# Which four of sixteen states are weighed on GpSimd: the fifth to eighth of a group, or the first four, with ScalarE copying their sum

## The chip, the cores and the metric

One core of one Trainium2 chip runs the whole program. Its engines are TensorE (PE, with its weight loads PEld), VectorE (DVE), ScalarE (ACT), GpSimd (POOL) and SyncE (SP), which here only issues DMAs. The metric is the device time of one execution in microseconds (us), lower is better.

## The reference, cut to what matters

Two adaLN layers over 2048 tokens of width 512. The first has a masked linear layer and a gated FFN. The second has a selective state-space block (the part that is changed) and a small mixture of LoRA experts. The state-space block, with D_IN = 1024 channels and N = 16 states:

```
dt = softplus(ts @ W_dt.T + b_dt)          # (tokens, 1024)
def step(state, inp):                      # over the tokens, in order
    dA = exp(dt_t[..., None] * A)
    state = state * dA + (dt_t * u_t)[..., None] * B_t[:, None, :]
    y = einsum('bdn,bn->bd', state, C_t)   # weigh the 16 states by C and add
    return (state, y)
y = ys + x * D
y = y * silu(gate)
return y @ W_out.T
```

## The kernel before, in words

Everything is written by hand: each engine has its own program, and semaphores order them. An engine runs its own program strictly in the order of the code.

Layer 0 takes the first part of the span. Layer 1 works on eight chunks of 256 tokens. In iteration i the state-space scan of chunk i runs, and between its steps lie pieces of the previous chunk p (out projection, router, experts) and of the next chunk n (norm, x projection, convolution, gates, dt). An iteration has 32 slots (`STEPS`): two groups g of four blocks of 128 channels, and 16 states in each. This text calls slot s of a group, counted from its start, st; the first group's slots are 0 to 15 of the iteration, the second's 16 to 31. In each slot:

- POOL multiplies `dbu = dtu * b_all` for all four blocks (L1851) and adds the folded carry into two columns (L1855). It may be up to four slots ahead of the scans (`AHEAD`).
- ACT makes the decay `exp(dt * A)` in two halves (L1612) and between them copies the last column of the previous state into `carry` (L1625); then it does the pieces that its function `others` lists for the slot before.
- DVE runs two scans (L2023), one for each half, into `h[:, s % RING]`, of which there are three.
- PE transposes the state into the two banks `ps_h`, one for each 128 tokens (`turn_h`, L1411), and DVE then adds it, weighed by C, to the sum `acc` (`add_state`, L2041; for a group's first state L2038, which sets `acc`). This follows one slot behind the scan.

Four states of each group, st 4 to 7, go another way (`on_pool`): POOL multiplies the state by a broadcast C in place (`weigh_h`, L1873, three slots behind its scan and behind that slot's `dbu`), and PE adds the transposes of all four into `ps_h` itself (`add_h`, L1399), together with D times u (`init_acc`, L1387). DVE then adds that sum to `acc` once (`join_acc`, L2050). Meanwhile states 8 and 9 wait for the banks. DVE has no add in st 5 to 8, the sum in st 9 and two adds in st 10; PE turns state 10 at the end of its slot 10, behind the x projection of that slot.

A buffer `h` comes free when PE has turned it: the scan of slot s waits for the transposes of slot s - 3. DVE's `rms_apply` (L2088, L2091) in slot 22 waits for POOL's `rms_pow` (L1907, L1909), which stands behind the `dbu` of slot 24.

## Time and profile before

| | |
|---|---|
| Times of three runs | 1701.98, 1704.54, 1706.6 us (median 1704.54) |
| The profiled execution | 1702.61 us, of which its span is 1700.8 us |
| DVE busy over the span | 1300.6 us (76%) |
| PE busy over the span | 1421.5 us (84%) |
| POOL busy over the span | 1079.5 us (63%) |
| ACT busy over the span | 891.7 us (52%) |
| Chain that ended last | PE 28%, POOL 20%, DVE 14%, issue 6%, ACT 3% |

Busy is the time in which the engine ran an instruction; the rest of the span it waited or had nothing to do. The shares are averages over layer 0 and layer 1, which have different limits. A group of rows gives the count and the mean time of its instructions; a row of the timeline gives start, duration, line, output <- inputs, and in brackets how long the engine was idle before it and for whom it waited.

### The profile page before, as it was taken

What the parts mean: (1) busy time and instruction counts of PE and PEld (TensorE: products, weight loads), DVE (VectorE), ACT (ScalarE), POOL (GpSimd) and SP (SyncE); (2) the same over time, 40 slices, a digit from 0 to 9 for tenths busy, and PEclk for the clock granted to TensorE, in tenths of its full rate; (3) what the DMA queues carried; (4) which work ended last, traced back from release to release, by engine and by line L of the source; (5) the groups of instructions that cost most, each with busy time, mean ns of one, the idle gap of its engine ahead of it and who ended that gap; (6) DMA issues with size and microseconds to landing.
All of it is one profiled execution on the core that took longest, in us unless ns stands there. A gap on an engine that the chain in (4) does not pass through costs nothing.

```text
span 1700.8 us, 25246 instructions
## 1 busy us (share of the span) xinstructions
PE 1421.5 (84%) x8781; PEld 1010.4 (59%) x8781; DVE 1300.6 (76%) x1746; ACT 891.7 (52%) x2369; POOL 1079.5 (63%) x958
## 2 busy tenths in 40 slices
PE   6789999999997785987898789788788878977677
PEld 5566766777765564665476456456546645745443
DVE  5685655554422898988989989898898998989983
ACT  3333333243215657656666665765666566575441
POOL 0352332322232969968977995996897699599780
PEclk9699999999999898999999999999999999999587
DMA  9421221111001002001100200110110030010001
GB/s 313 154 100 54 78 100 50 50 32 32 26 30 63 1 1 72 16 1 51 50 1 14 87 1 1 60 41 1 51 50 1 2 99 1 1 63 26 1 0 38
DMA packets 32579, 77.20 MB, mean 45 GB/s; under 512 B 3826, under 2 KB 4914, under 8 KB 31940
## 3 DMA queue, kind: packets, MB, share of 16 engines
q1 hardware_dynamic: 32452, 75.59, 13.1%
q8 instruction: 70, 1.15, 0.3%
q14 instruction: 57, 0.47, 0.1%
HBM read 66.99 MB, written 8.59 MB: 44 GB/s over the span
## 4 chain that ended last, share of the span: by engine, by line
PE 28%; POOL 20%; DVE 14%; issue 6%; ACT 3%; DVEq 0%; POOLq 0%; ACTq 0%
POOL dbu L1851 10%; DVE h L2023 7%; PE ps_h L1411 6%; POOL h L1873 5%; DVE acc L2041 3%; PE ps_m L1374 3%; PE ps_o L1435 2%; PE ps_m L159 2%; PE ps_m L1350 2%; PE ps_m L161 2%; PE ps_m L160 2%; PE ps_h L1399 2%; ACT ps_a L1612 2%; POOL dt L1917 1%; PE ps_s L1374 1%
## 5 line engine op out<-in xcount | busy, mean ns | idle before, releaser
L1851 POOL TENSOR_TENSOR dbu<-dtu,b_all 128x1024 f32<-128x1024 f32 x256 | 603.6, 2358 | 144.7 <-DVE h L2023 131.8
L2023 DVE TENSOR_TENSOR_SCAN h<-ps_a,carry,dbu 128x512 f32<-128x512 f32 x512 | 627.4, 1268 | 47.3 <-PE ps_h L1399 33.3
L1612 ACT ACTIVATE ps_a<-dt,a_neg 128x256 f32<-128x256 f32 (+1 forms) x1024 | 442.9, 465 | 238.6 <-DVE h L2023 238.2
L1411 PE MATMUL ps_h<-ident,h 128*128 128x128 f32 x1536 | 243.6, 303 | 125.5 <-DVE acc L2041 91.3
L1411 PEld LDWEIGHTS ps_h<-ident,h 128*128 128x128 f32 x1536 | 189.7, 155 | 193.8 <-DVE h L2023 107.4
L2041 DVE SCALAR_TENSOR_TENSOR acc<-ps_h,c_cur,acc 128x512 f32<-128x512 f32 x352 | 246.2, 740 | 34.2 <-PE ps_h L1411 33.5
L709 POOL TENSOR_TENSOR hid_l<-hid,hid_h 128x256 f16<-128x256 f32 (+1 forms) x88 | 77.2, 880 | 158.4 <-ACT hid_h L600 158.3
L1873 POOL TENSOR_TENSOR h<-h,c_all 128x1024 f32<-128x1024 f32 x64 | 150.6, 2352 | 23.1 <-ACT carry L1625 22.8
L159 PE MATMUL ps_m<-h_h,wi_h 128*128 128x256 f16 x440 | 125.5, 285 | 47.2 <-DVE u L2069 23.0
L592 ACT ACTIVATE sil<-ps_gu 128x256 f32<-128x256 f32 (+1 forms) x88 | 33.9, 385 | 180.9 <-PE ps_gu L161 180.9
L161 PE MATMUL ps_m<-h_h,wi_l 128*128 128x256 f16 x440 | 125.7, 286 | 0.0
L160 PE MATMUL ps_m<-h_l,wi_h 128*128 128x256 f16 x440 | 125.2, 284 | 0.0
L1435 PE MATMUL ps_o<-wo,y 128*128 128x512 f32 x224 | 108.5, 613 | 3.1 <-DVE x L2127 2.9
L1399 PE MATMUL ps_h<-ident,h 128*128 128x128 f32 x512 | 70.4, 282 | 34.4 <-POOL h L1873 34.1
L159 PE MATMUL ps_gu<-h_h,g_h 128*128 128x256 f16 (+1 forms) x352 | 96.6, 274 | 1.7 <-DVE u_l L998 1.0
L161 PE MATMUL ps_gu<-h_h,g_l 128*128 128x256 f16 (+1 forms) x352 | 96.5, 274 | 0.0
L160 PE MATMUL ps_gu<-h_l,g_h 128*128 128x256 f16 (+1 forms) x352 | 96.5, 274 | 0.0
L159 PE MATMUL ps_gu<-h_h,u_h 128*128 128x256 f16 (+1 forms) x352 | 96.1, 273 | 0.0
L160 PE MATMUL ps_gu<-h_l,u_h 128*128 128x256 f16 (+1 forms) x352 | 96.1, 273 | 0.0
L161 PE MATMUL ps_gu<-h_h,u_l 128*128 128x256 f16 (+1 forms) x352 | 96.1, 273 | 0.0
L1374 PE MATMUL ps_m<-xw,diag_t 128*128 128x256 f32 x384 | 91.1, 379 | 0.0
L1625 ACT ACTIVATE carry<-h 128x4 f32<-128x4 f32 x255 | 52.7, 207 | 70.9 <-DVE h L2023 70.5
(334 smaller groups left out, 2838.5 us busy)
## 6 DMA issues: line engine op xcount, KB each, us to landing
b_all<-bt_scratch SPq DMA_DIRECT2D x32, 512.0 KB, 4.0
wm<-in_wmod SPq DMA_DIRECT2D x7, 1024.0 KB, 6.5
wo<-in_wmod SPq DMA_DIRECT2D x5, 1024.0 KB, 9.1
xa<-in_x SPq DMA_DIRECT2D x8, 512.0 KB, 4.5
stage<-in_W_in SPq DMA_DIRECT2D x4, 1024.0 KB
x_scratch<-x SPq DMA_DIRECT2D x8, 512.0 KB, 3.1
c_all<-bt_scratch SPq DMA_DIRECT2D x8, 512.0 KB, 3.5
x<-x_scratch SPq DMA_DIRECT2D x8, 512.0 KB, 3.6
```

Source lines behind the costliest of these rows:

```text
L159: pe.matmul(out, lh, rh, start=(first and k == 0), stop=False)
L160: pe.matmul(out, lh, rl, start=False, stop=False)
L161: mm = pe.matmul(out, ll, rh, start=False, stop=(last and k == n - 1))
L1374: pe.matmul(x_bank(m), diag_t[:, m, tap], xw[:, m % 2, tap:tap + CH], start=(tap == 0), stop=False)
L1399: tr = pe.matmul(ps_h[:, t, j * P:(j + 1) * P], h[:, s % RING, j, t * P:(t + 1) * P], W["ident"][:], is_transpose=True, start=(begin and j ...
L1411: tr = pe.transpose(ps_h[:, t, j * P:(j + 1) * P], h[:, s % RING, j, t * P:(t + 1) * P], W["ident"][:])
L1435: mm = pe.matmul(ps_o[:], y[:, k, tok], W["wo"][:, k], start=(k == 0), stop=(k == KI - 1))
L1612: ex = nc.scalar.activation(ps_a[:, j, j % 2:], dt[:, m, j % 2:], ACT.Exp, scale=a_neg[:, m, st:st + 1])
L1851: nc.gpsimd.tensor_tensor(dbu[:, s % AHEAD], dtu[:, g * DG:(g + 1) * DG], b_all[:, st, :].unsqueeze(1).to_broadcast([P, DG, CH]), ALU.mult ...
L1873: nc.gpsimd.tensor_tensor(h[:, s % RING], h[:, s % RING], c_all[:, s % NS - C_FROM, :].unsqueeze(1).to_broadcast([P, DG, CH]), ALU.mult).t ...
L2023: nc.vector.tensor_tensor_scan(h[:, s % RING, two].rearrange("p j t -> p (j t)"), ps_a[:, two].rearrange("p j t -> p (j t)"), dbu[:, s % A ...
L2041: op = nc.vector.scalar_tensor_tensor(part, ps_h[:, t], c_t, part, ALU.mult, ALU.add)
```

## The change

The weighed states are now the first four of each group, st 0 to 3. PE adds state 0 in slot 1, state 1 in slot 3, state 2 in slot 4 and state 3 in slot 5, each time near the end of the slot (`ADD_AT`); `init_acc` is in slot 3. ACT copies the sum of the two banks into `acc` (`join_acc`, after the exponentials of slot 6), so `acc` starts with it: the product that set `acc` and DVE's add of the sum are both gone, and state 0 no longer needs either. DVE adds state 4 at the end of slot 6, states 5 and 6 in slot 7, and from slot 8 on one a slot as before. There are four buffers `h` instead of three. To make place, `dtu` holds one group instead of two: POOL makes the second group's in slot 15 behind its `dbu`, and the next chunk's first half in slot 31 (before: slots 5 and 30). Some small pieces of ACT and POOL move by a few slots. The scratch in DRAM holds 20 rows of B and C a chunk in place of 24.

```
-C_FROM = 4
-C_TO = C_FROM + KC
+ADD_AT = {1: 0, 3: 1, 4: 2, 5: 3}
+JOIN_AT = 5
...
-    RING = 3
+    RING = 4
...
-    dtu = sb("dtu", [P, KI, CH], F32, c)
+    dtu = sb("dtu", [P, DG, CH], F32, c)
...
     def on_pool(s):
-        return C_FROM <= s % NS < C_TO
+        return s % NS < KC
...
         def turn_h(i, s):
             pe.wait_ge(S["scan_half"], half_at(i, s, 1))
             for t in range(TT):
-                bank_free(i, use_of_step(s), t, first)
+                bank_free(i, use_of_step(s), 1 if s % NS == KC else t, False)
...
-                if st < C_FROM:
-                    turn_h(i, s, first)
-                elif st in (C_TO + 1, C_TO + 2):
-                    turn_h(i, s - 1, False)
-                elif st > C_TO + 2:
-                    turn_h(i, s, False)
+                if st == JOIN_AT + 1:
+                    turn_h(i, s - 2)
+                elif st == JOIN_AT + 2:
+                    turn_h(i, s - 1)
+                elif st > JOIN_AT + 2:
+                    turn_h(i, s)
...
-                if st == C_TO - 1:
+                if st in ADD_AT:
+                    add_h(i, s - st + ADD_AT[st], first)
+                if st == 3:
                     init_acc(i, s // NS)
-                if C_FROM < st <= C_TO:
-                    add_h(i, s - 1)
-                if st == C_TO + 2:
-                    turn_h(i, s, False)
+                if st == JOIN_AT + 1:
+                    turn_h(i, s - 1)
+                if st == JOIN_AT + 2:
+                    turn_h(i, s)
...
+        def join_acc(i, g, first):
+
+            if not first:
+                act.wait_ge(S["y_mm"], (i - 1) * (KI // 2) + (g + 1) * (DG // 2))
+            for t in range(TT):
+                act.wait_ge(S["hT_done"], turned_at(i, use_of_join(g), t))
+                nc.scalar.activation(acc[:, t, g * DG * P:(g + 1) * DG * P], ps_h[:, t], ACT.Copy).then_inc(S["hT_used"], 1)
...
             if s == 0:
                 keep_c(i, first)
+            if s % NS == JOIN_AT:
+                join_acc(i, s // NS, first)
...
-            if s == 5:
+            if s == 8:
                 first_decay(i, 1)
-            if s == 6:
+            if s == 9:
                 d_u(i, 1)
...
+            pool.wait_ge(S["db_mul"], (n * 2 + g) * NS)
+            nc.gpsimd.tensor_tensor(dtu[:], dt[:, grp], u[:, grp], ALU.mult).then_inc(S["dtu_done"], 1)
...
-            if s == 3:
+            if n is not None and s == 3:
+                inv_std_a(n - 1)
+            if s == 7:
                 dt_add(i, 1, first)
-            if n is not None and s == 4:
-                inv_std_a(n - 1)
-            if s == 5:
-                dt_u(i, 1)
...
-            if s == 8:
+            if s == 12:
                 fold_carry(i, 1, first)
+            if s == NS - 1:
+                dt_u(i, 1)
...
-        def join_acc(i, g):
-            use = use_of_join(g)
-            for t in range(TT):
-                dve.wait_ge(S["hT_done"], turned_at(i, use, t))
-                dve.wait_ge(S["hT_used"], i * (USES * TT) + (use * TT + t - 1))
-                part = acc[:, t, g * DG * P:(g + 1) * DG * P]
-                nc.vector.tensor_tensor(part, ps_h[:, t], part, ALU.add).then_inc(S["hT_used"], 1)
...
+            if m == DG and not first:
+                dve.wait_ge(S["dtu_done"], n * 2)
...
-                if st == C_TO + 1:
-                    join_acc(i, s // NS)
...
-                if st == C_TO + 2:
+                if st == JOIN_AT + 2:
                     add_state(i, s - 2)
-                elif (st <= C_FROM or st > C_TO + 2) and not (first and s == 0):
-                    add_state(i if s else i - 1, (s - 1) % STEPS, first)
+                elif (st == 0 or st > JOIN_AT + 2) and not (first and s == 0):
+                    add_state(i if s else i - 1, (s - 1) % STEPS)
...
-                if st == C_TO + 2:
+                if st == JOIN_AT + 1:
+                    add_state(i, s - 2)
+                if st == JOIN_AT + 2:
                     add_state(i, s - 1)
```

The order of three engines' instructions shows where the work stands now. Line numbers of after differ: L2035 is the scan, L2048 the weighed add, L2089 and L2092 `rms_apply`, L2076 a gate's product; on POOL L1863 and L1867 are `dbu`, L1885 `weigh_h`, L1919 and L1921 `rms_pow`.

DVE in the second group before, from `rms_apply` in slot 22 to the two adds of slot 26:

```order
L2088 TENSOR_TENSOR ssn<-ps_s,rms 128x2x32
L2091 TENSOR_TENSOR ssn<-ps_s,rms 128x32 x2
L2023 SCALAR_TENSOR_TENSOR h<-ps_a,carry,dbu 128x512 x2
L2075 SCALAR_TENSOR_TENSOR sg<-th,ps_m 128x256
L2023 SCALAR_TENSOR_TENSOR h<-ps_a,carry,dbu 128x512 x4
L2050 TENSOR_TENSOR acc<-ps_h,acc 128x512 x2
L2023 SCALAR_TENSOR_TENSOR h<-ps_a,carry,dbu 128x512 x2
L2041 SCALAR_TENSOR_TENSOR acc<-ps_h,c_cur,acc 128x512 x4
```

And now, from the same `rms_apply` in slot 22 to the adds of slot 23:

```order
L2089 TENSOR_TENSOR ssn<-ps_s,rms 128x2x32
L2092 TENSOR_TENSOR ssn<-ps_s,rms 128x32 x2
L2048 SCALAR_TENSOR_TENSOR acc<-ps_h,c_cur,acc 128x512 x2
L2035 SCALAR_TENSOR_TENSOR h<-ps_a,carry,dbu 128x512 x2
L2048 SCALAR_TENSOR_TENSOR acc<-ps_h,c_cur,acc 128x512 x2
L2076 SCALAR_TENSOR_TENSOR sg<-th,ps_m 128x256
L2048 SCALAR_TENSOR_TENSOR acc<-ps_h,c_cur,acc 128x512 x2
```

The stretch without adds ended four slots behind `rms_apply` and now ends with it, and the DVE's add of the sum is gone.

POOL in the second group before, from the first `weigh_h` to the second:

```order
L1873 TENSOR_TENSOR h<-h,c_all 128x1024
L1921 TENSOR_TENSOR gap<-top 128x2
L1922 CAST at<-top_at 128x4
L1851 TENSOR_TENSOR dbu<-dtu,b_all 128x1024
L1855 TENSOR_TENSOR dbu<-dbu,fold 128x2
L1907 TENSOR_SCALAR mse<-msq 128x6
L1909 TENSOR_TENSOR rms<-mse,mhalf 128x6
L1873 TENSOR_TENSOR h<-h,c_all 128x1024
```

And now, from the fourth `weigh_h` on:

```order
L1885 TENSOR_TENSOR h<-h,c_all 128x1024
L1863 TENSOR_TENSOR dbu<-dtu,b_all 128x1024
L1867 TENSOR_TENSOR dbu<-dbu,fold 128x2
L1933 TENSOR_TENSOR gap<-top 128x2
L1934 CAST at<-top_at 128x4
L1863 TENSOR_TENSOR dbu<-dtu,b_all 128x1024
L1867 TENSOR_TENSOR dbu<-dbu,fold 128x2
L1919 TENSOR_SCALAR mse<-msq 128x6
L1921 TENSOR_TENSOR rms<-mse,mhalf 128x6
```

`rms_pow` stood behind one weighing of the group and now stands behind all four.

PE in the first group before, from the norm's transposes in slot 3 to the out projection of slot 6 (L1286 turns the norm, L1435 is the out projection):

```order
L1286 MATMUL ps_s<-ident,xn 128x128 x4
L1435 MATMUL ps_o<-wo,y 128x512 x2
L1286 MATMUL ps_m<-ident,xn 128x128 x4
L1435 MATMUL ps_o<-wo,y 128x512 x4
L1399 MATMUL ps_h<-ident,h 128x128 x8
L1435 MATMUL ps_o<-wo,y 128x512 x2
```

And now, with the states' transposes among them:

```order
L1286 MATMUL ps_s<-ident,xn 128x128 x4
L1435 MATMUL ps_o<-wo,y 128x512 x2
L1399 MATMUL ps_h<-ident,h 128x128 x8
L1387 MATMUL ps_h<-ident,ab 128x128 x8
L1286 MATMUL ps_m<-ident,xn 128x128 x4
L1435 MATMUL ps_o<-wo,y 128x512 x2
L1399 MATMUL ps_h<-ident,h 128x128 x8
L1435 MATMUL ps_o<-wo,y 128x512 x2
L1399 MATMUL ps_h<-ident,h 128x128 x8
L1411 MATMUL ps_h<-ident,h 128x128 x8
```

The transposes that free the buffers `h` now stand behind the out projections of the first group, where there were none in between.

## Rows read from the trace of the kernel before

**Rows 1.** The page's busy times over the whole span.

```profile
PE 1421.5 (84%) x8781; PEld 1010.4 (59%) x8781; DVE 1300.6 (76%) x1746; ACT 891.7 (52%) x2369; POOL 1079.5 (63%) x958
```

**Rows 2.** Windows: six iterations, chunks 1 to 6, from join to join.

```profile
723.95:1571.00 847.05, 691.87 (x4159) 488.80 (x4158) 760.59 (x972) 542.30 (x1490) 698.42 (x591) 0.96 0.09 30
```

**Rows 3.** Waits of DVE in that stretch: total, times, longest.

```profile
DVE acc L2041 <- PE ps_h L1411: 29.1, 24, 3.6
DVE h L2023 <- PE ps_h L1399: 23.5, 16, 2.4
DVE acc L2050 <- PE ps_h L1399: 16.7, 12, 1.8
```

**Rows 4.** Groups by line over the span: busy us, mean ns | idle before.

```profile
L2023 DVE TENSOR_TENSOR_SCAN h<-ps_a,carry,dbu 128x512 f32<-128x512 f32 x512 | 627.4, 1268 | 47.3 <-PE ps_h L1399 33.3 <-ACT ps_a L1612 5.5 <-ACT carry L1625 5.4
...
L2041 DVE SCALAR_TENSOR_TENSOR acc<-ps_h,c_cur,acc 128x512 f32<-128x512 f32 x352 | 246.2, 740 | 34.2 <-PE ps_h L1411 33.5
...
L2038 DVE TENSOR_SCALAR acc<-ps_h,c_cur 128x512 f32<-128x512 f32 x32 | 22.3, 740 | 0.0
...
L2050 DVE TENSOR_TENSOR acc<-ps_h,acc 128x512 f32<-128x512 f32 x32 | 20.7, 686 | 23.2 <-PE ps_h L1399 23.2
```

**Rows 5.** Timeline of DVE in chunk 3's first group, slots 8 to 11.

```profile
999.02 2.46 DVE L2023 TENSOR_TENSOR_SCAN h<-ps_a,carry,dbu 128x512 f32<-128x512 f32 x2 [0.64 <-ACT carry L1625]
...
1003.63 2.46 DVE L2023 TENSOR_TENSOR_SCAN h<-ps_a,carry,dbu 128x512 f32<-128x512 f32 x2 [1.57 <-PE ps_h L1399]
1007.26 1.29 DVE L2050 TENSOR_TENSOR acc<-ps_h,acc 128x512 f32<-128x512 f32 x2 [1.17 <-PE ps_h L1399]
1008.46 1.28 DVE L2054 BATCH_NORM_STATS2 stats<-x 128x6 f32<-128x512 f32 x2
...
1014.88 1.41 DVE L2041 SCALAR_TENSOR_TENSOR acc<-ps_h,c_cur,acc 128x512 f32<-128x512 f32 x2 [0.70 <-PE ps_h L1411]
...
1022.62 1.41 DVE L2041 SCALAR_TENSOR_TENSOR acc<-ps_h,c_cur,acc 128x512 f32<-128x512 f32 x2 [3.65 <-PE ps_h L1411]
```

**Rows 6.** Timeline of DVE in chunk 2's second group, slots 24 to 27.

```profile
930.46 2.46 DVE L2023 TENSOR_TENSOR_SCAN h<-ps_a,carry,dbu 128x512 f32<-128x512 f32 x2 [0.54 <-PE ps_h L1399]
935.36 2.46 DVE L2023 TENSOR_TENSOR_SCAN h<-ps_a,carry,dbu 128x512 f32<-128x512 f32 x2 [2.44 <-PE ps_h L1399]
939.63 1.29 DVE L2050 TENSOR_TENSOR acc<-ps_h,acc 128x512 f32<-128x512 f32 x2 [1.81 <-PE ps_h L1399]
940.84 2.45 DVE L2023 TENSOR_TENSOR_SCAN h<-ps_a,carry,dbu 128x512 f32<-128x512 f32 x2
```

**Rows 7.** Timeline of POOL in the same stretch.

```profile
924.82 0.19 POOL L1855 TENSOR_TENSOR dbu<-dbu,fold 128x2 f32<-128x2 f32 x1
...
926.76 2.35 POOL L1873 TENSOR_TENSOR h<-h,c_all 128x1024 f32<-128x1024 f32 x1
929.06 2.36 POOL L1851 TENSOR_TENSOR dbu<-dtu,b_all 128x1024 f32<-128x1024 f32 x1
...
931.65 2.35 POOL L1873 TENSOR_TENSOR h<-h,c_all 128x1024 f32<-128x1024 f32 x1
```

**Rows 8.** Timeline of ACT in chunk 3, slots 6 and 7.

```profile
993.89 0.57 ACT L1635 ACTIVATE h_h<-ps_m 128x512 f16<-128x512 f32 x1
...
996.44 1.69 ACT L1696 ACTIVATE ab<-u,d_vec 128x256 f32<-128x256 f32 x4
```

**Rows 9.** Timeline of PE in chunk 2, slots 17 to 19.

```profile
909.33 3.92 PE L1350 MATMUL ps_m<-u,wx 128*64 128x256 f32 x16
913.19 1.10 PE L1411 MATMUL ps_h<-ident,h 128*128 128x128 f32 x8
...
918.06 1.09 PE L1411 MATMUL ps_h<-ident,h 128*128 128x128 f32 x8
```

**Rows 10.** Windows: chunk 3's slots 18 to 20 (PEclk is the third figure from the end).

```profile
1050.00:1065.00 15.00, 14.76 (x103) 10.34 (x103) 13.82 (x23) 6.83 (x21) 8.04 (x10) 0.89 0.01 2
```

More of the change, by code:

```diff
@@ L1389, in init_acc, with add_h @@
             tr.then_inc(S["init_done"], 1)
-        def add_h(i, s):
-            begin, last = s % NS == C_FROM, s % NS == C_TO - 1
+        def add_h(i, s, first):
+            begin, last = s % NS == 0, s % NS == KC - 1
             pe.wait_ge(S["hc_done"], on_pool_before(i, s) + 1)
@@ L1396, in add_h @@
                 if begin:
-                    bank_free(i, use_of_join(s // NS), t, False)
+                    bank_free(i, use_of_join(s // NS), t, first)
                 for j in range(DG):
@@ L1404, in add_h, with turn_h @@
                 tr.then_inc(S["hc_used"], 1)
-        def turn_h(i, s, first):
+        def turn_h(i, s):
             pe.wait_ge(S["scan_half"], half_at(i, s, 1))
             for t in range(TT):
-                bank_free(i, use_of_step(s), t, first)
+                bank_free(i, use_of_step(s), 1 if s % NS == KC else t, False)
                 for j in range(DG):
@@ L1710, in tsb_in @@
             act.wait_ge(S["tsb_mm"], n + 1)
-            nc.scalar.activation(tsb[0:RDT + NS + C_TO, :], ps_s[0:RDT + NS + C_TO, 0:CH], ACT.Copy).then_inc(S["tsb_done"], 1)
+            nc.scalar.activation(tsb[0:RDT + NS + KC, :], ps_s[0:RDT + NS + KC, 0:CH], ACT.Copy).then_inc(S["tsb_done"], 1)
         def router_in(p):
@@ L1850, in db @@
                 pool.wait_ge(S["scan_half"], i * (2 * STEPS) + 2 * (s - AHEAD + 1))
-            nc.gpsimd.tensor_tensor(dbu[:, s % AHEAD], dtu[:, g * DG:(g + 1) * DG],
+            nc.gpsimd.tensor_tensor(dbu[:, s % AHEAD], dtu[:],
                                     b_all[:, st, :].unsqueeze(1).to_broadcast([P, DG, CH]), ALU.mult).then_inc(S["db_mul"], 1)
@@ L1967, in others @@
                 weigh(p)
-            if s == 8:
+            if s == 12:
                 fold_carry(i, 1, first)
+            if s == NS - 1:
+                dt_u(i, 1)
             if n is not None and s == STEPS - 3:
                 dt_add(n, 0)
-            if n is not None and s == STEPS - 2:
+            if n is not None and s == STEPS - 1:
                 dt_u(n, 0)
-            if n is not None and s == STEPS - 1:
                 fold_carry(n, 0)
@@ L2026, in scans, with add_state @@
                                              carry[:, s, 2 * half:2 * half + 1], ALU.mult, ALU.add).then_inc(S["scan_half"], 1)
-        def add_state(i, s, first=False):
+        def add_state(i, s):
             g, st, use = s // NS, s % NS, use_of_step(s)
-            if st == 0 and not first:
-                dve.wait_ge(S["y_mm"], (i - 1) * (KI // 2) + (g + 1) * (DG // 2))
             for t in range(TT):
@@ L2036, in add_state @@
                 c_t = c_cur[:, t, st:st + 1]
[L2037 to L2050 removed]
+                dve.wait_ge(S["hT_used"], i * (USES * TT) + (use * TT + t - 1))
+                op = nc.vector.scalar_tensor_tensor(part, ps_h[:, t], c_t, part, ALU.mult, ALU.add)
+                op.then_inc(S["hT_used"], 1)
         def statistics(n, src, st, ag):
@@ L2064, in low, with make_u @@
                                     ALU.subtract).then_inc(lo, 1)
-        def make_u(n, m):
+        def make_u(n, m, first=False):
             dve.wait_ge(S["tanh_done"], value(n, KI, m))
+            if m == DG and not first:
+                dve.wait_ge(S["dtu_done"], n * 2)
             nc.vector.scalar_tensor_tensor(u[:, m], th[:, m % 2], 1.0, x_bank(m), ALU.add, ALU.mult).then_inc(S["u_done"], 1)
@@ L2116, in first_dt @@
             dve.wait_ge(S["dt_done"], 1)
-            nc.vector.tensor_tensor(dtu[:, 0:DG], dt[:, 0:DG], u[:, 0:DG], ALU.mult).then_inc(S["dtu_done"], 1)
+            nc.vector.tensor_tensor(dtu[:], dt[:, 0:DG], u[:, 0:DG], ALU.mult).then_inc(S["dtu_done"], 1)
         def make_y(i, m):
@@ L2209, in _ @@
         for m in range(KI):
-            make_u(0, m)
+            make_u(0, m, True)
         mean_squares(0)
```

30 lines of the change are left out of this document (12 added, 18 removed).

## The prediction, made before the changed kernel ran

> **What bounds the kernel now.** I read the page's busy times first, then windows over the six alike iterations, then the waits of VectorE in that stretch, and last the timelines of single groups. Over the whole span VectorE is busy 76% and POOL 63% [rows 1], which is a mean over two layers. In the six iterations of chunks 1 to 6 the reader should see another picture: 847.05 us, of which VectorE works 760.59 and POOL 698.42 [rows 2]. An iteration takes 141.2 us, with 126.8 us of VectorE's work, and 86.5 us / 6 = 14.4 us in which it waits. So VectorE bounds layer 1, and a change is worth what it takes from its work plus what it takes from these 14.4 us. The waits have three main names: the weighed add behind PE's transposes (29.1 us), the scan behind `add_h` (23.5) and the join behind `add_h` (16.7) [rows 3]. All three belong to the stretch in which four states are weighed.
>
> Why it waits there: POOL needs 929.06 - 926.76 = 2.30 us for a weighing and 931.65 - 929.06 = 2.59 us for a slot's `dbu` with its small add [rows 7], so 4.89 us for a slot with both. VectorE needs 2.37 us for a slot's two scans, and has no add there. Its scans start 935.36 - 930.46 = 4.90 us apart [rows 6]: POOL's pace. With three buffers `h` the scan of slot s also waits for the weighing of s - 3 and PE's eight transposes behind it.
>
> **The change, part by part.** I count from T, the end of a group's first scan. The first weighing starts at T + 0.5.
>
> *Work.* The join on VectorE goes: 1008.46 - 1007.26 = 1.20 us a group [rows 5]. Setting `acc` goes, but state 0 to 3 are weighed now and all twelve others are added; before it was one set and eleven adds, and both kinds take 740 ns [rows 4]. So only the join counts: 16 x 1.20 = 19.2 us, of it 2.4 in each iteration.
>
> *The join on ACT.* The nearest row is a copy of one bank in 0.57 us, to half-width numbers [rows 8]; I take 0.6 each, 1.2 for two. Bounds: 0.5 and 0.75 each. Behind it on ACT stand a gate's tanh or the copy of the norm (slot 5's list), and the exponentials of slot 7, and VectorE's scan waits for those.
>
> *Fourth buffer.* A scan now waits for the weighing of s - 4, which stands on POOL ahead of this slot's own `dbu`. So where PE is in time the fourth buffer leaves `dbu` as the bound.
>
> *First group.* POOL: four weighings (9.2), the `dbu` of slots 4 to 7 (10.4), the norm's small steps (1.5): the fourth weighing ends at T + 19.0. VectorE until then has its statistics (1.5), the last add (1.3), five scans (11.8), two products y, four gates and others: some 19 us, so it hardly waits on POOL. PE has four gate tiles, four out projections of 1.7 to 1.9 us, and the transposes behind them. By my walk through the slots the third `add_h` ends at 20.1, where the scan of slot 6 waits 0.75 us for it, and the fourth at 22.8. ACT waits for that, copies until 23.6 and then copies the norm until 24.2, which VectorE needs in slot 6: 1.65 us. ACT's normalise and `d_u` (1.69 us [rows 8]), which now meet slots without an add, cost 0.25 and 0.45; the turn of state 7 behind an out projection and an x tile 0.3. With some 0.6 for latencies that is 4.0 us. Before it was 0.64 + 1.57 + 1.17 + 0.70 + 3.65 = 7.7 us [rows 5]. The 3.65 is PE's turn of state 10, which stood behind an x tile that waits for VectorE's own slot 11; now the late turns are those of states 5 and 7, ahead of any tile that waits so.
>
> *Second group.* VectorE has an add, u, and y in slots 16 to 18. PE turns y, does `wx` in 3.92 us [rows 9] and reaches the first `add_h` at T + 10.9; then a gate tile and the router (3.6 us, between the transposes at 913.19 and 918.06 [rows 9]). ACT takes the router's output at 14.8 and tanh after it, so VectorE waits 1.8 us in slot 20 for the gate. The scans of slots 21 and 22 wait 0.6 and 0.65 for `add_h`, the gate of slot 22 another 1.25 (tanh stands behind the join on ACT). Then comes `rms_apply`. POOL's `rms_pow` stood behind one weighing and now stands behind four: 0.5 + 4 x 2.30 + 5 x 2.59 + 0.3 (`gap`) + (926.76 - 925.0 = 1.7) [rows 7] = T + 24.7. VectorE is ready at 24.7 after those waits, so this costs nothing more, but if the others shrink it is what comes late next: it ends the stretch at T + 24.7 in any case. PE turns state 20 at 25.05, and the add of it starts at 25.2. The waits sum to 1.8 + 0.6 + 0.65 + 1.25 + 0.3 + 0.5 = 5.1. Before, this group and the rest of the iteration had 14.4 - 7.3 = 7.1 us (the first group varies by some 1 us over the chunks), of which 0.54 + 2.44 + 1.81 stand in [rows 6].
>
> *PE's clock.* In slots 18 to 20 the granted clock is 0.89 of full over 15 us [rows 10], so the array ran about 3.3 us of it at 1.2 GHz and the rest at 2.4, after a wait. PE now waits some 3 us ahead of the second y of slot 17. I put 1.0 us an iteration on it (between 0, since the row shows that one such drop is there already, and 1.65, half of 3.3). The Trainium skill, "TensorE: Matmul & The Clock Gate", Part 1, says that the array falls to half its rate when it has been idle and comes back after it was kept busy. By that rule there would be a drop in each second group inside the critical stretch; at the upper bound the sum would be 4 us less of a gain. The row agrees that there are drops, not where the new ones would lie.
>
> *Moved without cost.* `dtu` in slots 15 and 31 (2.36 us of POOL) stands right ahead of the next group's first `dbu`, and that is needed four slots later; POOL runs its work from slot 16 to the next slot 3 without a pause by T + 62.3, and VectorE is there at T + 64.4. Were that cover gone, each would cost up to 2.4 us. The new wait of u(4) for `dtu` has 6 us of slack. ACT's dt steps in slots 24 to 28 no longer lie in a stretch at POOL's pace; 1.2 us for these and the experts' late sum.
>
> **The sum.** Waits in an iteration: 4.0 + 5.1 + 1.0 + 1.2 = 11.3 for 14.4, so -3.1; work -2.4; together -5.5, times six -33. The first and the last chunk bring their four joins, -4.8, and I give their waits nothing. That is -37.8 on the profiled execution of 1702.61 us: 1664.8. The median lies 1.9 higher, so 1666. For this kernel 0.3%, or 5 us, is about what can be told from no change.
>
> **The rivals.**
> - *Only the work goes.* The waits move but stay 14.4 us: the join chain (fourth weighing, transposes, ACT's copy, turn, add) takes the place of `add_h` and VectorE's join. For it: the chain has one more engine in it. Against: 3.65 us had a cause of its own. 1704.5 - 19 = 1685. Chance 0.25.
> - *The waits fall to 8 us.* PE and ACT get through without the small waits and only the POOL-bound end is left. Another 3.3 x 6 = 20 us: 1647. Chance 0.10.
> - *PE is late.* The transposes that free `h` and open the banks stand behind gates, router and out projections. PE's stretch from the second y to the fourth `add_h` is 17.8 us long and ends only 0.15 us ahead of need, so every further us there is one of VectorE's. From 5.5 us an iteration on it decides. Were the stretch wholly at 1.2 GHz it would be about 12 us longer: 7 x (12 - 5.5) = +45, 1750. For it: short light slots now hold the same PE work. Against: over the six iterations the clock is 0.96 [rows 2] and PE has 155 us free. Slower in some such way: 0.07, mostly at 1712 to 1730.
> - *Nothing measurable*: gain and PE's lateness cancel, 1704. Chance 0.05.
>
> **How the numbers follow.** The forecast, 1655 to 1678, has 0.53. With the first rival above it and half of the second below, 1647 to 1692 holds somewhat over 8 in 10. Faster by over 0.3% is the forecast and the first two rivals: 0.53 + 0.25 + 0.10 = 0.88; same 0.05; slower 0.07.
>
> **What would show it.** VectorE's busy time falls by about 22 us (the joins' 20.7 [rows 4]). The six iterations take 135 to 137 us each, with 11 us of waiting; the 3.65 us wait of the eleventh slot is gone. A new wait of `rms_apply` for POOL's `rms` or just under it appears in slot 22, and one for ACT in slots 6 and 20. The scans' waits for PE shrink to the small ones of slots 6, 21 and 22. I am wrong if the waits of add and scan together are as large as before, if ACT's join starts later than T + 25, or if POOL shows no waits for scans in slots 26 to 31 and its `dbu` makes the scans wait.

## The result: 1660.87 us, and the profile after

| | before | after |
|---|---|---|
| Times | 1701.98 to 1706.6 us, median 1704.18 (4 runs) | 1657.41 to 1664.34 us, median 1660.87 (4 runs) |
| Profiled execution, its span | 1702.61, 1700.8 us | 1660.69, 1658.5 us |
| Granted clock over the span | 0.937 | 0.943 |

The ratio is 0.9746, with a 95% interval of 0.9721 to 0.977: 43 us faster. 1666.0 was forecast, with a range of 1647 to 1692.

First the page's busy times, which answer to [rows 1]:

```profile
PE 1399.8 (84%) x8781; PEld 1000.2 (60%) x8781; DVE 1281.2 (77%) x1714; ACT 900.7 (54%) x2401; POOL 1078.1 (65%) x958
```

VectorE works 1300.6 - 1281.2 = 19.4 us less, in 32 instructions fewer. The span fell by 42.3 us. So more than half of the gain is waiting that went, and it must be looked for in the six alike iterations.

For these I take the same mark in both kernels, `rms_apply` in slot 22 (L2088 before, L2089 after), which stands once in each of chunks 0 to 6. This is the view of one line's instructions, with the first and the last start; from the one to the other are six iterations. The first row is of the kernel before, the second of the one after:

```profile
L2088 DVE TENSOR_TENSOR ssn<-ps_s,rms x7: 224/225/228, 645.5 to 1493.5; 128x64 f32<-128x64 f32 x7
```

```profile
L2089 DVE TENSOR_TENSOR ssn<-ps_s,rms x7: 216/217/225, 643.6 to 1460.8; 128x64 f32<-128x64 f32 x7
```

An iteration fell from 848.0 / 6 = 141.3 us to 817.2 / 6 = 136.2. The windows between these marks, before and after (the second answers to [rows 2]; after the times and the counts of the five engines stand the clock, the DMA share and GB/s):

```profile
645.50:1493.50 848.00, 691.14 (x4182) 493.39 (x4180) 761.98 (x978) 545.62 (x1500) 697.54 (x586) 0.95 0.09 30
```

```profile
643.60:1460.80 817.20, 681.86 (x4177) 490.41 (x4178) 749.09 (x953) 551.73 (x1521) 698.55 (x586) 0.95 0.10 31
```

The third engine is VectorE: its work fell by 12.9 us, 2.15 an iteration, and its waiting from 86.0 to 68.1 us, so from 14.3 to 11.35 an iteration. The clock stayed at 0.95. What it waits for now, in the same window of the kernel after (answers to [rows 3]):

```profile
DVE sg L2076 <- ACT th L1668: 18.3, 17, 1.8
DVE h L2035 <- ACT carry L1627: 15.6, 18, 1.9
DVE h L2035 <- PE ps_h L1399: 15.4, 24, 0.9
DVE h_l L2062 <- ACT h_h L1637: 7.9, 6, 1.5
DVE x L2128 <- PE ps_o L1435: 5.1, 5, 1.0
DVE acc L2048 <- PE ps_h L1411: 2.9, 13, 0.3
```

Two of the three names of [rows 3] are all but gone: the weighed add waited 29.1 us and now waits 2.9, and the join's 16.7 went with the join. The third, the scans behind `add_h`, is at 15.4. In their place ScalarE is named, for 41.8 us in all: a gate's tanh (L1668), the carry (L1627) and the fp16 copy (L1637).

The two places where these waits lie, on VectorE, first the first group of chunk 4 (its T is 1091.4; answers to [rows 5]):

```profile
1100.22 0.42 DVE L2076 SCALAR_TENSOR_TENSOR sg<-th,ps_m 128x256 f32<-128x256 f32 x1 [0.32 <-ACT th L1668]
1101.08 2.46 DVE L2035 TENSOR_TENSOR_SCAN h<-ps_a,carry,dbu 128x512 f32<-128x512 f32 x2 [0.44 <-ACT carry L1627]
...
1108.48 0.69 DVE L2128 TENSOR_TENSOR x<-ps_o,x 128x512 f32<-128x512 f32 x1 [1.01 <-PE ps_o L1435]
1109.52 2.46 DVE L2035 TENSOR_TENSOR_SCAN h<-ps_a,carry,dbu 128x512 f32<-128x512 f32 x2 [0.35 <-PE ps_h L1399]
...
1113.42 2.46 DVE L2035 TENSOR_TENSOR_SCAN h<-ps_a,carry,dbu 128x512 f32<-128x512 f32 x2 [0.86 <-PE ps_h L1399]
1117.15 0.69 DVE L2062 TENSOR_TENSOR h_l<-ps_m,h_h 128x512 f16<-128x512 f32 x1 [1.27 <-ACT h_h L1637]
```

Then the second group of chunk 3 (T is 1024.95; answers to [rows 6]):

```profile
1037.79 2.46 DVE L2035 TENSOR_TENSOR_SCAN h<-ps_a,carry,dbu 128x512 f32<-128x512 f32 x2 [1.94 <-ACT carry L1627]
1042.10 0.42 DVE L2076 SCALAR_TENSOR_TENSOR sg<-th,ps_m 128x256 f32<-128x256 f32 x1 [1.85 <-ACT th L1668]
...
1044.22 2.46 DVE L2035 TENSOR_TENSOR_SCAN h<-ps_a,carry,dbu 128x512 f32<-128x512 f32 x2 [0.47 <-PE ps_h L1399]
...
1047.63 2.46 DVE L2035 TENSOR_TENSOR_SCAN h<-ps_a,carry,dbu 128x512 f32<-128x512 f32 x2 [0.63 <-PE ps_h L1399]
1051.02 0.42 DVE L2076 SCALAR_TENSOR_TENSOR sg<-th,ps_m 128x256 f32<-128x256 f32 x1 [0.93 <-ACT th L1668]
1051.36 0.22 DVE L2089 TENSOR_TENSOR ssn<-ps_s,rms 128x64 f32<-128x64 f32 x1
```

ScalarE in the same stretch shows who stands behind whom:

```profile
1036.52 0.38 ACT L1703 ACTIVATE ss_t<-ps_m 64x256 f32<-64x256 f32 x1 [2.54 <-PE ps_m L1350]
...
1041.39 0.40 ACT L1717 ACTIVATE rl<-ps_o 128x272 f32<-128x272 f32 x1 [2.59 <-PE ps_o L1472]
1041.69 0.38 ACT L1668 ACTIVATE th<-ps_m 128x256 f32<-128x256 f32 x1
...
1049.63 1.08 ACT L1740 ACTIVATE acc<-ps_h 128x512 f32<-128x512 f32 x2 [1.88 <-PE ps_h L1399]
1050.60 0.39 ACT L1668 ACTIVATE th<-ps_m 128x256 f32<-128x256 f32 x1
```

The scan of slot 20 waits 1.94 us because ScalarE, ahead of the carry, waits for TensorE's `wx` (L1350). The two waits of L2076 are a tanh that stands behind the router's copy (L1717) and one that stands behind the new join (L1740). The join of both banks takes 1.08 us. And on GpSimd, `rms_pow` in that chunk:

```profile
1048.29 1.35 POOL L1921 TENSOR_TENSOR rms<-mse,mhalf 128x6 f32<-128x6 f32 x1
```

It ends at 1049.64, which is T + 24.7; its reader L2089 comes at 1051.36 and does not wait. Of the seven readings only the first, in chunk 0, waited (0.55 us).

### The profile page after: what moved, and what is told of

Its sections match the earlier page's. It is cut to its first block, busy times and chain, and to the rows that moved or that the text cites. A ratio compares the mean times of both kernels' runs of the same rounds, so it can differ in the third digit from the quotient of the medians.

```text
span 1658.5 us, 25273 instructions
## 1 busy us (share of the span) xinstructions
PE 1399.8 (84%) x8781; PEld 1000.2 (60%) x8781; DVE 1281.2 (77%) x1714; ACT 900.7 (54%) x2401; POOL 1078.1 (65%) x958
## 4 chain that ended last, share of the span: by engine, by line
PE 32%; DVE 20%; issue 8%; ACT 6%; POOL 3%; DVEq 0%; ACTq 0%; POOLq 0%
DVE h L2035 11%; DVE acc L2048 6%; PE ps_h L1411 4%; PE ps_o L1435 4%; PE ps_h L1399 3%; PE ps_m L159 3%; PE ps_m L161 3%; PE ps_m L160 3%; PE ps_m L1374 2%; ACT ps_a L1614 2%; PE ps_m L1350 2%; POOL dbu L1863 2%; POOL h L1885 1%; PE ps_s L1374 1%; PE ps_s L1421 1%
## 5 line engine op out<-in xcount | busy, mean ns | idle before, releaser
L2035 DVE TENSOR_TENSOR_SCAN h<-ps_a,carry,dbu 128x512 f32<-128x512 f32 x512 | 627.6, 1268 | 42.8 <-ACT carry L1627 18.4
L1863 POOL TENSOR_TENSOR dbu<-dtu,b_all 128x1024 f32<-128x1024 f32 x256 | 603.5, 2358 | 48.5 <-DVE h L2035 34.9
L1411 PE MATMUL ps_h<-ident,h 128*128 128x128 f32 x1536 | 230.5, 293 | 128.8 <-DVE acc L2048 114.1
L1411 PEld LDWEIGHTS ps_h<-ident,h 128*128 128x128 f32 x1536 | 182.7, 149 | 186.2 <-DVE h L2035 152.3
L2048 DVE SCALAR_TENSOR_TENSOR acc<-ps_h,c_cur,acc 128x512 f32<-128x512 f32 x384 | 268.2, 740 | 7.4 <-PE ps_h L1411 7.2
L1885 POOL TENSOR_TENSOR h<-h,c_all 128x1024 f32<-128x1024 f32 x64 | 150.6, 2354 | 13.2 <-ACT carry L1627 13.2
L1435 PE MATMUL ps_o<-wo,y 128*128 128x512 f32 x224 | 108.4, 607 | 0.2
L717 POOL COPY x<-x 128x1024 f32<-128x1024 f32 x8 | 8.7, 1093 | 120.3 <-issue 120.3
L1627 ACT ACTIVATE carry<-h 128x4 f32<-128x4 f32 x255 | 52.8, 207 | 54.2 <-DVE h L2035 54.1
```

What stands on the lines that cost most here:

```text
L1411: tr = pe.transpose(ps_h[:, t, j * P:(j + 1) * P], h[:, s % RING, j, t * P:(t + 1) * P], W["ident"][:])
L1435: mm = pe.matmul(ps_o[:], y[:, k, tok], W["wo"][:, k], start=(k == 0), stop=(k == KI - 1))
L1863: nc.gpsimd.tensor_tensor(dbu[:, s % AHEAD], dtu[:], b_all[:, st, :].unsqueeze(1).to_broadcast([P, DG, CH]), ALU.mult).then_inc(S["db_mul" ...
L1885: nc.gpsimd.tensor_tensor(h[:, s % RING], h[:, s % RING], c_all[:, s % NS, :].unsqueeze(1).to_broadcast([P, DG, CH]), ALU.mult).then_inc(S ...
L2035: nc.vector.tensor_tensor_scan(h[:, s % RING, two].rearrange("p j t -> p (j t)"), ps_a[:, two].rearrange("p j t -> p (j t)"), dbu[:, s % A ...
L2048: op = nc.vector.scalar_tensor_tensor(part, ps_h[:, t], c_t, part, ALU.mult, ALU.add)
```

## The experiments

Each is timed against the kernel before on the same chip, whose median was 1703.16 in the first four (17 runs), 1703.37 in the second four and 1703.89 in the last four (9 runs each). The change itself was timed in a fourth set, so it is best compared with an experiment by their ratios. "An iteration" is again the time between the marks of slot 22 by six, of one profiled execution each: 141.3 before.

| kernel | median us | ratio, 95% interval | an iteration |
|---|---|---|---|
| the change | 1660.87 | 0.9746 (0.9721 to 0.977) | 136.2 |
| e1_three_buffers | 1780.39 | 1.0448 (1.0432 to 1.0464) | 153.0 |
| e2_before_four_buffers | 1700.62 | 0.9979 (0.9968 to 0.9991) | 141.3 |
| e3_join_on_vector | 1685.76 | 0.9897 (0.9879 to 0.9915) | 140.0 |
| e4_before_turn_first | 1685.18 | 0.9889 (0.9874 to 0.9903) | 138.6 |
| e5_adds_early | 1646.58 | 0.9655 (0.9625 to 0.9684) | 133.8 |
| e8_rms_later | 1668.42 | 0.9786 (0.9763 to 0.981) | 137.3 |
| e6_adds_and_rms_early | 1639.26 | 0.9628 (0.9604 to 0.9653) | 133.4 |
| e7_join_behind | 1639.94 | 0.9628 (0.9607 to 0.965) | 133.4 |
| e9_wx_first | 1656.22 | 0.9719 (0.9697 to 0.9741) | 135.2 |
| e10_router_in_behind | 1659.55 | 0.9741 (0.9716 to 0.9765) | 136.3 |
| e12_wx_first_adds_early | 1638.74 | 0.9612 (0.9589 to 0.9635) | 133.6 |
| e11_all_early | 1640.95 | 0.9631 (0.9608 to 0.9653) | 133.5 |

### The parts of the change

**e1_three_buffers**: the changed kernel with three buffers.

```
-    RING = 4
+    RING = 3
```

> The changed kernel with three buffers h in place of four, nothing else. My theory: the scans of slots 5 and 6 (20 to 22) then wait for the transposes of the third and fourth weighed state, which PE does only at the end of slots 4 and 5; from the trace of after these end about T + 20.7 and T + 23.3 in the first group and similar, one slot later, in the second, against scans that start at T + 16.6 and 20.5. That is some 3 us a first group and 4 us a second, 7 x 7 = about 50 us more than after: 1700 to 1715 us. Rival (the buffer is hardly needed, the join off VectorE and the freed turn did it): within 10 us of after, 1661 to 1671.

**e2_before_four_buffers**: the kernel before with four, and with the one-group `dtu` that makes room for it.

```
-    RING = 3
+    RING = 4
...
-    dtu = sb("dtu", [P, KI, CH], F32, c)
+    dtu = sb("dtu", [P, DG, CH], F32, c)
...
```

GpSimd's product `dtu` moves to slots 15 and 31 with it, as in the change.

> The kernel before with four buffers h and the one-group dtu that makes place for the fourth; the weighed states stay the fifth to eighth. My theory: the stretch without adds still ends with the join behind the fourth weighing, so a scan that starts earlier only makes the wait for the join longer: gain 0 to 1 us an iteration, 1696 to 1705 us. Rival (the fourth buffer is the gain): the 23.5 us of scan waits of the six iterations go, 1675 to 1685.

The fourth buffer gives the old order some 3 us and is worth 120 us to the new one: both expectations for e1 were far off, and e1 is slower than the kernel before. In e1 VectorE's scans wait 156.3 us for `add_h` in the six iterations (the waits of VectorE there):

```profile
DVE h L2035 <- PE ps_h L1399: 156.3, 42, 5.5
```

Two rows of VectorE and four of TensorE, in one first group of e1, show the circle:

```profile
1169.71 2.46 DVE L2035 TENSOR_TENSOR_SCAN h<-ps_a,carry,dbu 128x512 f32<-128x512 f32 x2 [3.73 <-PE ps_h L1399]
...
1177.87 2.46 DVE L2035 TENSOR_TENSOR_SCAN h<-ps_a,carry,dbu 128x512 f32<-128x512 f32 x2 [4.45 <-PE ps_h L1399]
```

```profile
1168.47 1.04 PE L1399 MATMUL ps_h<-ident,h 128*128 128x128 f32 x8
...
1172.87 1.12 PE L1286 MATMUL ps_m<-ident,xn 128*128 128x128 f32 x4 [2.49 <-DVE sg L2076]
1173.78 3.01 PE L1435 MATMUL ps_o<-wo,y 128*128 128x512 f32 x4
1176.63 1.04 PE L1399 MATMUL ps_h<-ident,h 128*128 128x128 f32 x8
```

With three buffers the scan of slot 5 waits for the `add_h` at the end of TensorE's slot 4 (1168.47). TensorE's slot 5 waits for VectorE's gate, which stands behind that scan (1172.87), then does its out projection, and only then the `add_h` that the scan of slot 6 waits for (1176.63). So the two engines work by turns. A part of the loss is TensorE's clock: behind its wait of 2.49 us the out projection of slot 5 took 3.01 us, where the same four matmuls take 1.88 in the kernel after, and the granted clock over the span was 0.917 against 0.943. The old order, with three buffers too, had 23 us of scans waiting for `add_h`. In e2 the scans no longer wait for `add_h` (23.0 us before), but the join does, 43.6 us where it was 17.3: the buffer alone moved the wait to the next thing that needs GpSimd's fourth weighing. From mark to mark e2 gained nothing (847.8 us, 848.0 before), so its 3 us lie outside the six iterations.

**e3_join_on_vector**: the changed kernel with the join back on VectorE, as two copies ahead of the add of state 4.

```
-            if s % NS == JOIN_AT:
-                join_acc(i, s // NS, first)
...
+                nc.vector.tensor_copy(acc[:, t, g * DG * P:(g + 1) * DG * P], ps_h[:, t]).then_inc(S["hT_used"], 1)
```

> The changed kernel, but VectorE copies the sum of the weighed states into acc, right ahead of its add of state 4. My theory: 16 x 1.2 to 1.3 us of VectorE's work come back, and in exchange the waits behind ACT's copy (1.27 us for the norm in the first group, 0.93 for the gate in the second) go for the most part: 8 to 16 us above after, 1669 to 1677. Rival one (ACT's copy costs as much in waits as it saves in work): 1658 to 1664. Rival two (only VectorE's work counts): 1680 or more.

It gives back 25 us, more than the work and more than the 8 to 16 that were expected; the time lies in the range of the second rival, but work alone does not make it. From mark to mark VectorE is busy 764.21 us (749.09 after, +15.1) and waits 75.5 (68.1, +7.4). The waits for the fp16 copy (7.9 us) went, as the theory said, and those for the tanh fell from 18.3 to 12.8; but those of the weighed add rose from 2.9 to 22.4. One of these is a round trip:

```profile
1127.88 1.28 DVE L2043 COPY acc<-ps_h 128x512 f32<-128x512 f32 x2
1130.12 1.60 DVE L2053 SCALAR_TENSOR_TENSOR acc<-ps_h,c_cur,acc 128x512 f32<-128x512 f32 x2 [0.96 <-PE ps_h L1411]
```

The copy frees the banks only when VectorE comes to it, so TensorE turns state 4 late and the add right behind the copy waits 0.96 us. ScalarE did the same copy while VectorE scanned.

**e4_before_turn_first**: the kernel before, where in slot 10 TensorE turns state 10 ahead of the x tile instead of behind it.

```
-                if st == C_TO + 2:
-                    turn_h(i, s, False)
...
+                if st == C_TO + 2:
+                    turn_h(i, s, False)
                 if n is not None:
                     for m in XT_AT.get(s, ()):
                         x_tile(n, m, False)
```

> The kernel before, with PE's turn of state 10 moved ahead of the x projection's tile in slot 10 of the first group. My theory: the wait of 3.65 or 2.5 us of the add in slot 11 goes, 3.1 us on the mean, once an iteration, six or seven times: 19 to 22 us faster, 1682 to 1686. Rival (the wait only passes to the x tile and the convolution behind it): within 5 us of before, 1699 to 1704.

18 us: the time lies in the expected range, the gain just under the 19 to 22 us. Two rows of TensorE in the kernel before, chunk 3, show what stood ahead of the turn of state 10, the x tile (12 matmuls) and its first one's wait:

```profile
1019.03 0.35 PE L159 MATMUL ps_m<-h_h,wi_h 128*128 128x256 f16 x1 [1.81 <-DVE u L2069]
...
1021.52 1.53 PE L1411 MATMUL ps_h<-ident,h 128*128 128x128 f32 x8
```

The x tile waited for VectorE's `u`, which is the last thing that VectorE did before its own wait of 3.65 us [rows 5]. In e4 that wait is not there, and the waits of the weighed add fell from 29.1 to 11.5 us over the six iterations, while those of the scans for `add_h` rose from 23.0 to 27.4:

```profile
DVE acc L2041 <- PE ps_h L1411: 11.5, 19, 1.1
```

So two lines in another order do alone what nearly half of the whole change does. The change with the join back on VectorE (e3, ratio 0.9897) is no faster than e4 (0.9889); what brings it from there to 0.9746 is the join on ScalarE.

### What is left of the waits

**e5_adds_early**: the changed kernel, TensorE adding states 1 to 3 a slot earlier.

```
-ADD_AT = {1: 0, 3: 1, 4: 2, 5: 3}
+ADD_AT = {1: 0, 2: 1, 3: 2, 4: 3}
```

> The changed kernel with TensorE adding states 1, 2 and 3 one slot earlier (ADD_AT 1:0, 2:1, 3:2, 4:3); same work. In chunk 4 of the changed kernel GpSimd's weighed states end at 1101.44, 1106.35 and 1111.26, so each is there by the end of TensorE's earlier slot. Theory (what is left of the waits around the sum is set by the slot in which TensorE adds): the waits of the scans for L1399 (0.35 and 0.86 in the first group, 0.47 and 0.63 in the second), and those of VectorE's L2062 (1.27) and L2076 (0.93) behind ScalarE's copy of the sum, mostly go: 2.5 to 4.5 us an iteration, 1627 to 1645 us. Rival (the other pieces of TensorE and ScalarE are the bound, and the waits come back a slot later): 1653 to 1664 us. Rival two (transposes now stand ahead of the x projection and the router and delay them): 1666 us or more.

**e8_rms_later**: the changed kernel with `rms_pow` a slot later.

```
-                if n is not None and s == WX_AT + 7:
+                if n is not None and s == WX_AT + 8:
```

> The changed kernel with GpSimd's rms_pow one slot later, behind the dbu of slot 25. In the changed kernel's chunk 3 rms_pow ended at 1049.64 and VectorE reached its reader at 1051.36 without a wait, so 1.7 us are to spare; a dbu with its fold is 2.6 us. Theory (the slack is 1.7 us): a wait of about 0.9 us an iteration, 1664 to 1671 us. Rival (VectorE has other waits behind it that take this up, or c_cur is not needed soon): 1658 to 1663 us. Rival two (there was no slack, the row hides a wait of ScalarE of the same length): 2.6 us an iteration, 1677 us or more.

**e6_adds_and_rms_early**: e5, and `rms_pow` at `WX_AT + 6`.

> e5 with GpSimd's rms_pow one slot earlier too, behind the dbu of slot 23. Theory: if the adds of e5 bring VectorE to the reader of rms_pow 2 us earlier in slot 22, its slack of 1.7 us is used up, and this gives back what is left over: 0 to 0.8 us an iteration below e5. Rival: no difference from e5 within 0.3%.

e5 takes another 14 us. The scans' waits for L1399 (15.4 us) and those for the fp16 copy (7.9) are gone from VectorE's waits; the out projection of slot 4 took back 4.1 of them:

```profile
DVE x L2128 <- PE ps_o L1435: 9.2, 6, 1.9
DVE acc L2048 <- PE ps_h L1411: 5.1, 22, 0.3
```

That is 2.4 us an iteration, just under what was expected, and the median lies 1.6 above that range.

In e8 an iteration takes 1.1 us more, where 2.6 - 1.7 = 0.9 was expected. In chunks 1, 2 and 4 VectorE does wait 1.00, 0.82 and 1.03 us for `rms`: there `rms_pow` ended 1.7 us ahead of need in the kernel after, as was said. In chunks 3, 5 and 6 it does not wait for it at all, since `wx` took 5.9 to 6.2 us there and the scan of slot 20 waited 3.0 to 3.3. So the slack is shown, and that the total came out near 0.9 is in part luck.

In e6 an iteration is 0.3 us shorter than in e5 (2.0 us in six), and the wait of 2.1 us for `rms` in chunk 0 is gone. The other 3.4 us of the 7.4 between the two spans lie ahead of the first scan, where both kernels are the same: the first scan starts at 548.7 in e5 and at 545.3 in e6. The intervals of the two ratios overlap.

**e7_join_behind**: e6 with ScalarE's join behind the other pieces of its slot.

```
-            if s % NS == JOIN_AT:
-                join_acc(i, s // NS, first)
...
             if p is not None and s == MID_AT + 1:
                 mid_in(p)
+            if s % NS == JOIN_AT:
+                join_acc(i, s // NS, first)
```

> e6 with ScalarE's copy of the sum behind the other pieces of its slot (the fp16 copy in slot 6 and a gate's tanh in slot 22) instead of ahead of them. The copy is 1.08 us. Theory: VectorE's L2062 and L2076 come up to 1.1 us earlier and the transposes of state 4 up to 0.6 us later; with the sum there early the transposes have room, so 0 to 1 us an iteration below e6. Rival: the transposes of state 4 end late for VectorE's add of slot 6, and what the one gains the other loses: within 0.3% of e6, or up to 0.6 us an iteration above.

No difference from e6. The waits for the tanh fell from 19.2 to 13.0 us and those of the weighed add rose from 5.6 to 13.0, as the rival said.

**e9_wx_first**: the changed kernel with `wx` ahead of the turn of y in slot 17. **e12_wx_first_adds_early**: the same edit on e6.

```
-                for m in YA_AT.get(s, ()):
-                    turn_y(i, m)
                 if n is not None and s == WX_AT:
                     wx(n)
+                for m in YA_AT.get(s, ()):
+                    turn_y(i, m)
```

> The changed kernel with TensorE's x projection (wx, slot 17) ahead of the transposes of the gated output in the same slot. In the changed kernel TensorE idled 3.16 us for VectorE's y at 1030.60, then did these transposes (1.09 us) and only then wx (4.86 us), and the scan of slot 20 waited 1.94 us behind ScalarE's copy of wx's result; wx's last input was there at 1029.94. Theory (the order on TensorE, not its clock, makes that wait): wx ends about 1.5 us earlier, the wait falls to 0.3 to 0.6 us, but the gate and router behind it end only 0.6 us earlier, so L2076's wait of 1.85 grows to about 2.7: net 0.6 us an iteration, 1652 to 1659 us. Rival one (the router's wait is not tied to it): 1.5 us an iteration, 1646 to 1651 us. Rival two (a slower granted clock for the first matmuls eats it): 1659 us or more.

> e6 (adds and rms_pow one slot earlier) with wx ahead of the transposes of the gated output. In e6 the wait of the scan of slot 20 is 2.31 and that of L2076 behind it 1.84, and no scan waits for L1399. Theory as in e9: net 0.6 to 1.0 us an iteration below e6, 1631 to 1635 us. Rival: 1.5 us an iteration, 1627 us or less.

e9's time fits the first theory, but its mechanism was wrong. The waits for the carry fell from 15.6 to 3.9 us and those for the tanh from 18.3 to 6.8; the latter should have grown. In their place came one that I had not thought of (waits of VectorE in e9, mark to mark):

```profile
DVE y L2122 <- PE ps_s L1421: 17.8, 6, 3.1
```

VectorE's product y of slot 18 needs the turn of y, which now stands behind `wx`. `wx` itself became a little slower too, 5.26 us on the mean of the seven where it was 4.94. Its 16 matmuls as one row each, in chunk 3 of the kernel after, of e9 and of e12:

```profile
1031.62 4.86 PE L1350 MATMUL ps_m<-u,wx 128*64 128x256 f32 x16
```

```profile
1027.04 5.35 PE L1350 MATMUL ps_m<-u,wx 128*64 128x256 f32 x16 [2.55 <-DVE u L2070]
```

```profile
1020.64 6.42 PE L1350 MATMUL ps_m<-u,wx 128*64 128x256 f32 x16 [2.55 <-DVE u L2070]
```

e12 is the same as e6, and both of its expectations fell. From e6 to e12 the waits for the carry and the tanh fell by 24.3 us over the six iterations; y's wait brought 19.5, the out projection of slot 4 another 3.2 and `rms` 1.8. The 6.42 us of `wx` is no cause of it: it stands in this chunk alone, and the mean is 5.27 where e6 has 5.12. Why the out projection comes later for VectorE in e12 than in e6 is open.

**e10_router_in_behind**: the changed kernel, ScalarE's router copy behind the gate's tanh. **e11_all_early**: that edit on e12.

```
-            if p is not None and s == RA_AT + 1:
-                router_in(p)
             if n is not None:
                 for m in at_slot(GA_AT, s):
                     gate_tanh(n, m)
+            if p is not None and s == RA_AT + 1:
+                router_in(p)
```

> The changed kernel with ScalarE's copy of the router's sums (L1717) behind the gate's tanh (L1668) of the same slot. The gate's matmuls ended at 1039.3, the router's at 1041.2, and the tanh stood behind the copy. Theory: L2076's wait of 1.85 in slot 20 goes, but TensorE's sums for the scans of slots 21 and 22 are not earlier, so their waits of 0.47 and 0.63 grow to 2 to 2.5: net 0.3 us an iteration or less, 1656 to 1662 us. Rival (TensorE runs ahead when VectorE frees its banks earlier): 1.0 to 1.8 us an iteration, 1646 to 1653 us.

> e12 with ScalarE's copy of the router's sums behind the gate's tanh too. With the sum a slot early, nothing on TensorE stands behind the tanh that VectorE would wait for before slot 22. Theory: L2076's wait of slot 20 goes to 0.9 us or less, and the choice of experts waits up to 0.5 us for the copy: 1.5 to 2.5 us an iteration below e6, 1619 to 1628 us. Rival (GpSimd's weighed states or TensorE's own work set the time of the second group): 1630 us or more.

e10 changes nothing, much as was expected: the waits for the tanh fell from 18.3 to 6.6 us, those for L1399 rose from 15.4 to 20.1 (the longest to 1.6, not to 2 or more), those for the carry from 15.6 to 17.8, and the choice of experts now waits 6.7 for the router's copy. In e11 the theory fell: the rival named a time of 1630 or more, and 1640.95 is no better than e12. The largest wait there is again y's for TensorE, 19.4 us. These waits suggest, though no run isolates it, that the second group is bound at this point by TensorE's string of y, `wx`, gate and router behind VectorE's slot 17, in whichever order VectorE meets it.

## Why the prediction was right, step by step

**That VectorE bounds the iteration**, and that a change is worth its work and its waits: right. 2.15 us of work and 3.0 us of waiting went, 5.1 in all; forecast were 2.4, 3.1 and 5.5. An iteration takes 136.2 us (135 to 137 forecast) with 11.35 us of waiting (11.3).

**The work of the join pair**, 19.2 us: VectorE's busy time fell by 19.4 (I had written 22 in what would show it, and that was too much). e3 puts it back and shows that a join on VectorE costs some 6 us beyond its work (25 - 19), in waiting.

**The cause of the 3.65 us wait**, TensorE's turn of state 10 behind an x tile: shown by e4, 18 us of the 43. That was the argument against the rival of only the work, and 19.2 of work with 18 of this is already 37; the medians' difference is 43.3. e3 has the whole change but the join's move, and is 17 us below the kernel before; that these are the same microseconds as e4's 18 is argued, since the two parts were not run together without the rest.

**The first group**, 4.0 us of waits: 4.9 in chunk 4 (0.32 + 0.44 + 0.24 + 1.01 + 0.35 + 0.86 + 1.27 + 0.16 + 0.28). The scan of slot 6 waits 0.86 (0.75 forecast), the reader of the ScalarE copy 1.27 (1.65). The fourth weighing ends at T + 19.9, where 19.0 was forecast; that figure holds three `dbu`, not the four (10.4 us) that the text names beside it. The join starts at T + 24.0, not 22.8; and 22.8 with two copies of 0.6 would have ended at 24.0, not at 23.6. Not foreseen was the 1.01 us for the out projection.

**The second group**, 5.1 and 1.0 for the clock: 6.2 in chunk 3 (the five shown, 5.8, and 0.4 in the choice of experts). The gate of slot 20 waits 1.85 (1.8 forecast), the scans of slots 21 and 22 0.47 and 0.63 (0.6 and 0.65), the gate of slot 22 0.93 (1.25). The 1.0 for the clock lies in one place, the scan of slot 20, which waits 1.9 us in every chunk. The 3.92 us of [rows 9], from which the walk started, is only one of two lengths: before, `wx` took 3.83 to 3.93 us in four of seven iterations and 4.80 or 4.81 in the other three, and in the kernel after 4.79 to 5.03 in all. On the mean that is 4.28 and 4.94, so 0.66 us an iteration at a lower clock; the rest of the 1.9 is that `wx` ends late for other reasons. `rms_pow` ends at T + 24.7, to the tenth, and its reader comes 1.7 us later, where I had it level. The join of that group starts at T + 24.7 too, just inside the T + 25 from which I would have been wrong.

GpSimd is no longer the pace of the stretch: TensorE's waits for its weighed states, 20.6 us from mark to mark before, are not among its waits now. But GpSimd has less to spare over the whole iteration, since its `dbu` waited 28.4 us for scans where it waited 106.7.

**The fourth buffer**: "where PE is in time the fourth buffer leaves `dbu` as the bound" is too weak a sentence. e1 shows that without it TensorE is never in time. I costed the buffer by what the old order would gain from it (e2: 3 us), and not by what the new order would lose without it. As both came together, the sum was not hurt. (One of the transposes that free `h` stood between the out projections before too, as the order of PE before shows; now two do, and a third stands behind the last of them.)

**The mis-sized term** is "the first and the last chunk bring their four joins, -4.8, and I give their waits nothing". From the start to the first mark the span lost 1.9 us, and from the last mark to the end it fell from 207.3 to 197.7: 11.5 us where 4.8 were forecast. These windows, of before and of after:

```profile
0.00:645.50 645.50, 582.37 (x3911) 423.23 (x3911) 373.84 (x565) 245.93 (x613) 236.31 (x242) 0.96 0.21 72
1493.50:1700.80 207.30, 148.03 (x691) 93.80 (x690) 164.77 (x206) 100.19 (x259) 145.60 (x132) 0.81 0.07 26
```

```profile
0.00:643.60 643.60, 579.62 (x3919) 421.56 (x3919) 366.13 (x554) 247.22 (x617) 242.83 (x245) 0.96 0.21 72
1460.80:1658.50 197.70, 138.35 (x687) 88.19 (x685) 165.98 (x209) 101.70 (x265) 136.73 (x129) 0.85 0.08 27
```

The two have to be read together: now VectorE's adds of a group stand behind the mark of slot 22, where some stood ahead of it. Ahead of the first mark VectorE's work fell by 7.7 us and its waiting rose by 5.8; behind the last its work rose by 1.2 and its waiting fell from 42.5 to 31.7. Together that is 6.5 us of work, where 4.8 were forecast, and 5.0 of waiting, where nothing was. Behind the last mark the scans' waits for `add_h` fell from 7.8 to 1.4, the join's 4.5 to none, and the last norm's for the out projection from 7.0 to 5.4. In the six iterations 30.8 us went where 33 were forecast; the two errors partly cancel, and some 5 us are left by which the forecast was too slow.

**The rivals**: that only the work goes falls with e4 and with the waits; the waits at 8 us are what e5 and e6 come near (e5: 802.6 - 749.0 = 53.6 us, 8.9 an iteration). That TensorE is late did not come, though e1 is this rival with its circle closed: 11.7 us an iteration above before, more than the 5.5 from which it decides.

**The best kernels** are e6, e7, e11 and e12, the same by their intervals: 1639 to 1641 us, by the ratios 3.7 to 3.9% below before and 1.2 to 1.4% below the change. e6 is the simplest of them: the change, with the adds and `rms_pow` a slot earlier.

## What to carry to other kernels

Before a change is judged by the work it saves, look at the longest single wait and ask what stands ahead of the late instruction on its own engine: here a piece that itself waited for the engine that was kept waiting, and to put it behind gave 18 us. A buffer's worth depends on the order of the work: test it in the new order, where it was worth 120 us, and not in the old, where it was worth 3. And when a wait is taken away on an in-order engine, read what comes next in its row first: of e5's 23 us of waits removed some 15 arrived, and of e9's 23 some 6.
